# Order of the next norm in the attention steps, of one small transpose, and of four matmul groups in an attention and feed-forward layer

## The chip, the cores and the metric

One core of one Trainium2 chip runs the whole program in one launch. The metric is the time on the device in microseconds (us). Engines: PE is TensorE (matmuls and transposes), DVE is VectorE, ACT is ScalarE, POOL is GpSimd, SP is SyncE, whose queue issues most of the transfers (DMA).

## The reference

x has 2048 tokens of 1024 numbers, all float32. It is a layer with two halves:

```python
x = x + attention(layernorm(x))
x = x + ffn(layernorm(x))
# attention: q, k, v = h @ w.T + b, 32 heads of 32; per TOKEN, over the heads:
#   scores = q[h] . k[t] / sqrt(32); probs = softmax over t; context = probs @ v
# ffn: w1, w2, w3 are quantized to 16 levels (NF4) with one scale for 64 weights,
#   and dequantized; out = (silu(x @ w1.T) * (x @ w2.T)) @ w3.T, hidden size 2752
```

The attention mixes the 32 heads of one token, not the tokens. So the work of 128 tokens is independent of that of all others.

## The kernel before

**Attention.** The tokens are taken in 16 steps of 128 rows (n = 0 to 15, T = 16). In step n the projections of rows n are made, while the attention of the rows of step n-1 is finished (their second half of V's evacuation and the scores, softmax and mixing), the norm of the rows n+1 is made, and the second norm (ahead of the feed-forward part) is made of rows n-2. Each engine has its own program; they meet at semaphores only. Steps 2 to 13 are written as a loop of two steps on SP and DVE, and in full on the others.

- PE in one step (`step` in `tensor`, L1072): the first half of the scores (64 products of 32x32 for 16 of 32 tokens of a quadrant, recorded as 128), Q's first half (16 matmuls of 128x512 into one bank), the second half of the scores, Q's second half, then the wait for `normed` and the eight transposes of the next rows (`turn`, L281), K in two halves with the first mix product between them, the second mix product, and V.
- DVE in one step (`step` in `vector`, L821): V's second evacuation of the rows before, the transposition of V, one look at feed-forward weights (an absmax over blocks of 64, L813), the statistics of the next rows (`norm_stats`), the statistics of the second norm (`moments2`, whose last instruction is L263), Q's first evacuation (L799), `center(n, 0)` (row maxima and subtraction for the first half of the scores, L934 and L936), `norm_apply` (L275: (x - mean) * rstd on 128x1024 numbers in SBUF), a look, the flip of the first half of the probabilities (`flip_probs`, L951), the second norm (L942), `center(n, 1)`, and so on.
- ACT makes the exponential of each half (L1028), splits the transposed rows into a high half (L287), and makes one level of the first quantized weights after another (L1021, L1023).
- POOL in one step (`step` in `gpsimd`): the residual of rows n-2 (L766), `inv_std` (the power -0.5 of the next rows' variance, L271), `inv_std2` (the same for the second norm, L770, which waits for DVE's L263), then `add_level` three times (L760: one more level is added to 128x1024 weights). Level 0 of a unit of weights needs no addition: the first call has none in steps 1, 6 and 11.

The next rows' norm needs DVE's statistics and POOL's power. PE's transposes wait for it:

```python
def norm_apply(dve, n, slot):
    dve.wait_ge(rstd_ready, n + 1)
    nc.vector.tensor_scalar(x_nat[:, slot], x_nat[:, slot], mean_var[:, 0:1], rstd[:, 0:1],
                            ALU.subtract, ALU.mult).then_inc(normed, 1)
```

**From attention to feed-forward.** Parts of the feed-forward program run inside steps 14 and 15 and the tail. Each engine's feed-forward program is a generator; a call of `next(feed)` or `next(ahead)` runs it to its next `yield`. PE's parts are: the transposition of the four maxima of the weights (L1924, waits for `ff_max`), inside V of step 14; the spread of the four maxima to all partitions (L1927, waits for `ff_max_all`, DVE's L1754 and L1755), at the end of step 14. DVE reads the spread in step 15 (L1759); POOL's power L1553 follows.

**The opening.** Round 0 of the feed-forward part has a form of its own. Gate and up of the first tile of hidden units are made for the token blocks 0 and 1 (512 tokens each), 24 matmuls to each of the four products. The scores and mixes of the very last rows (step "T") are put between these matmuls: `gate_up` gets a slot number, counts on by one for each matmul, and `attend_last` puts the halves of the scores behind the slots 0 and 8 and the halves of the mix behind the slots 40 and 56. The first mix waits for `flip_probs(T, 0)` of DVE, the second for `flip_probs(T, 1)`. Product (m, sb_): m is 0 for gate and 1 for up, sb_ is the token block. Gate waits for the transposed weights of gate, up for those of up, and both for the tokens of the block (`x2_in`). SP's queue has, in this order, the transposition of up's weights (`turn_early(1)`), the store of x2's rows and the load of token block 1 (`load_tokens(1)`).

ACT makes silu of the two gates in the opening in a fixed order with the signs from which DVE sums up the next weights:

```python
silu(0, 0, 0, P)
silu(0, 0, 1, P)
compare(0, opening_steps[7:11], FULL)
hidden_hi(0, 0, 0, P)
```

DVE in the tail (`tail` in `vector`) has the statistics of rows 14, `center(T, 0)`, the second norm of rows 14, `flip_probs(T, 0)`, three sums, `center(T, 1)`, one sum, `flip_probs(T, 1)`, `sum_rows`, two sums, `weigh(15, 0)`, the three sums of the signs 7 to 9, `weigh(15, 1)`, the context's flip, `hidden_value` of block 0 and so on. The residual (POOL), the second norm and the turning of the last rows follow.

**Rounds.** From then on 11 rounds, each with gate and up of two tiles for four token blocks, and the down product of 16 token tiles. The weights of the next tiles are quantized meanwhile: signs on ACT (L1584), sums on DVE (L1716, L1718), scales and low halves on POOL, transposition by DMA.

Of the kernel before, what the change touches and what calls it, by code (L numbers as in the profile page):

```python
# [175 lines left out]
def attention(nc, g):  # L176
# [13 lines left out]
    with ExitStack() as mine:  # L190
# [74 lines left out]
        def norm_stats(dve, n, slot, loaded):  # L265
            dve.wait_ge(x_in[slot], 16 * loaded)
            moments(dve, x_nat[:, slot], stats, mean_var, var_eps, var_ready)
# [5 lines left out]
# [4 lines that stand above are left out]
# [513 lines left out]
        def vector(dve, feed):  # L790
            def evacuate(n, u, it, m, h):
                i = 2 * m + h
                cols = slice(h * BANK, (h + 1) * BANK)
                if m > 0 and h == 0:
                    dve.wait_ge((None, q_ready, k_ready)[m], n + 1)
                if m == 0 and h == 0 and not (it is None and n == 0):
                    dve.wait_ge(v_ready, n)
                dve.wait_ge(projected, 6 * n + i + 1)
                nc.vector.scalar_tensor_tensor(qkv[:, cols], bank[:, (6 * u + i) % PROJ_RING], un_scale[:, i:i + 1],  # L799
                                               bias[:, m, cols], ALU.mult, ALU.add).then_inc(evacuated, 1)  # L800
# [15 lines left out]
            def step(n, u, it, project=True, normalize=True, attend=True, end=True, feed=None, ahead=None):  # L816
                todo = looks(n, u, it)

                def look():
                    if todo:  # L820
                        look_at(*todo.pop(0))  # L821

                if it is not None:
                    seq.at(before_loop + it * (2 * MARKS) + u * MARKS)
                if attend:
                    evacuate(n - 1, 1 - u, it, 2, 1)
                    turn_v(n)
                    look()
                if feed:
                    next(feed)  # L830
                if normalize:
                    norm_stats(dve, n + 1, 1 - u, (n + 1) // 2 + 1 if it is None else it + 2 + u)
                if end:
                    moments2(n - 2)
                if normalize and not attend:
                    norm_apply(dve, n + 1, 1 - u)
                    look()
                if project:
                    evacuate(n, u, it, 0, 0)
                if attend:  # L840
                    center(n, 0)
                if feed:
                    next(feed)
                if normalize and attend:
                    norm_apply(dve, n + 1, 1 - u)
                look()
                if attend:
                    flip_probs(n, 0, end)
                if end:
                    norm2(n - 2)  # L850
                if attend:
                    center(n, 1)
                if project:
                    evacuate(n, u, it, 0, 1)
                if feed:
                    next(feed)
                if normalize:
                    split_lo(dve, n + 1, xT_lo[:, 1 - u], xT_hi[:, 1 - u], x_hi_done, x_lo_done)
                if attend:
                    flip_probs(n, 1, end)  # L860
                if project:
                    dve.wait_ge(evacuated, 6 * n + 2)
                    nc.vector.transpose(qT[:].rearrange("p t h u -> p h t u"),
                                        qkv[:].rearrange("p (h d) -> p h d", d=HD)).then_inc(q_ready, 1)
                if feed:
                    next(feed)
                if attend:
                    sum_rows()
                look()
                if project:  # L870
                    evacuate(n, u, it, 1, 0)
                look()
                if ahead:
                    dve.wait_ge(absmax_done, 3 * FT + 3 + 2)
                    next(ahead)
                if attend:
                    weigh(n - 1, 0)
                if project:
                    evacuate(n, u, it, 1, 1)
                    dve.wait_ge(evacuated, 6 * n + 4)  # L880
                    nc.vector.transpose(kT[:].rearrange("p t h u -> p h t u"),
                                        qkv[:].rearrange("p (h d) -> p h d", d=HD)).then_inc(k_ready, 1)
                if project:
                    evacuate(n, u, it, 2, 0)
                if feed:
                    next(feed)
                if attend:
                    weigh(n - 1, 1)
                    flip_context(n - 1)
                look()  # L890
                if it is None and n == 0:
                    invert_first()
                if ahead:
                    next(ahead)
                if it is not None:
                    assert seq.off == MARKS
                    if u == 1:
                        seq.at(before_loop + LOOP * 2 * MARKS)
# [22 lines left out]
            def turn_v(n):  # L921
                dve.wait_ge(evacuated, 6 * n)
                nc.vector.transpose(vT[:].rearrange("p t d u -> p d t u"),
                                    qkv[:].rearrange("p (d h) -> p d h", h=HEADS)).then_inc(v_ready, 1)
# [124 lines left out]
        def tensor(pe, feed_program):  # L1049
# [22 lines left out]
            def step(n, u, it, project=True, normalize=True, attend=True, end=True, feed=None, ahead=None,  # L1072
                         with_lo=False):
                def score_second():
                    score_part(n, end, HALF, QUAD)

                def mix_first():
                    mix_part(n, 0, HALF)

                def ahead_half():  # L1080
                    next(ahead)

                if project:
                    pe.wait_ge(x_lo_done, 2 * n + 2)
                    if attend:
                        score_part(n, end, 0, HALF)
                    project_one(n, u, it, 0, with_lo, score_second if attend else None)
                if normalize:
                    pe.wait_ge(normed, n + 2)
                    turn(x_nat[:, 1 - u], x_turned)  # L1090
                if project:
                    project_one(n, u, it, 1, with_lo, mix_first if attend else None)
                    if attend:
                        mix_part(n, HALF, QUAD)
                    project_one(n, u, it, 2, with_lo, ahead_half if ahead else None)
                if ahead:
                    next(ahead)

            def score_part(n, end, first, last):

                for t in range(first, last):
                    half = t // HALF
                    if t == 0:
                        pe.wait_ge(k_ready, n)
                    if t == 0:
                        pe.wait_ge(q_ready, n)
                    if t % HALF == 0 and end and scores_of(n) is scores:
                        pe.wait_ge(ctx_read, 2 * n + half - 3)
                    for rows in quadrants:
                        ins = nc.tensor.matmul(scores_of(n)[rows, t], qT[rows, t // 2, :, t % 2], kT[rows, t // 2, :, t % 2], start=True, stop=True)  # L1110
                    if t % HALF == HALF - 1:
                        ins.then_inc(scores_done, 1)
# [52 lines left out]
def feed_forward(nc, g):  # L1165
# [26 lines left out]
    with ExitStack() as mine:  # L1192
# [655 lines left out]
        def tensor(pe):  # L1848
# [62 lines left out]
            def body(r, sizes, opening=False):  # L1911
                for w in range(4):
                    if opening and w == 0:
                        for at, (m, sb_) in enumerate(((0, 0), (0, 1), (1, 0), (1, 1))):
                            gate_up(r, 0, sb_, P, (m,), True, 3 * C * at)
                        continue
                    gate_up(r, w // 2, w % 2 * 2, sizes[w // 2], opening=opening)
                    gate_up(r, w // 2, w % 2 * 2 + 1, sizes[w // 2], opening=opening)
                pe.wait_ge(w_ready, (r * 6 + 6) * 32)
                for st in range(T):  # L1920
                    down(r, st, sizes[0:GROUP])
# [34 lines left out]
```

## Time and profile before

| | us |
|---|---|
| median of 3 runs | 1895.01 (1889.67 to 1895.59) |
| the profiled execution, its own time | 1894.59 |
| its span, first to last instruction | 1892.7 |
| PE busy | 1831.2 |
| DVE busy | 1729.0 |
| ACT busy | 1378.0 |
| POOL busy | 1252.9 |
| granted TensorE clock, mean | 0.993 |

The profile is of one execution. Busy times are sums of instructions. A row of the timeline has the start in us, the duration in us, the engine, the line of the kernel, the operation with the tile written and those read, the shapes, the number of instructions that the row joins, and in square brackets how long the engine had been idle before and who released it. Starts of neighbouring instructions overlap their predecessors' ends by some 0.07 us on DVE, and matmuls overlap by design. The granted clock is given as a share of 2.4 GHz.

### The profile page before, as it was taken

The numbers are of one execution on the slowest core, as the hardware profiler recorded it, in microseconds if no ns is written. First come the engines' busy times: TensorE is split into PE (matmuls) and PEld (weight loads), VectorE is DVE, ScalarE is ACT, GpSimd is POOL, SyncE is SP. The second block draws the span as 40 slices with busy tenths as digits, with TensorE's granted clock in tenths as the row PEclk, the third lists the DMA queues.
The fourth block names the chain that finished last, engine by engine and source line by source line (L and its number), as shares of the span: only waits on it lengthen the run. The fifth ranks groups of instructions, "written<-read, shape, count | busy, mean of one in ns | idle before, by whom it ended". The sixth has DMA issues, their size and how long they took to land. (4 is left out here: it accounts for less than half of the span.)

```text
span 1892.7 us, 42748 instructions
## 1 busy us (share of the span) xinstructions
PE 1831.2 (97%) x16470; PEld 884.2 (47%) x16470; DVE 1729.0 (91%) x1848; ACT 1378.0 (73%) x1523; POOL 1252.9 (66%) x706
## 2 busy tenths in 40 slices
PE   6899999999989999999999999999999999999998
PEld 6555555555434344444444444444444444444443
DVE  6799999999888999999999999999999999999985
ACT  7233333333359898898998988989989889898881
POOL 0134534534647887977878779778787787787961
PEclk9999999999999999999999999999999999999999
DMA  9346666665587131221122212212211221131115
GB/s 322 123 128 188 169 173 198 170 174 157 133 215 239 41 66 45 45 62 49 44 52 47 56 44 50 61 44 50 61 44 44 50 61 44 44 65 42 39 29 190
DMA packets 252925, 182.76 MB, mean 97 GB/s; under 512 B 177792, under 2 KB 220800, under 8 KB 252800
## 3 DMA queue, kind: packets, MB, share of 16 engines
q1 hardware_dynamic: 221600, 167.28, 31.8%
q10 hardware_dynamic: 31200, 13.64, 3.5%
q8 instruction: 100, 1.64, 0.4%
q14 instruction: 25, 0.20, 0.0%
HBM read 114.29 MB, written 24.12 MB: 73 GB/s over the span
## 5 line engine op out<-in xcount | busy, mean ns | idle before, releaser
L1718 DVE SCALAR_TENSOR_TENSOR bank<-signs,bank 128x1024 f32<-128x1024 int8 (+2 forms) x756 | 919.9, 1217 | 53.2 <-ACT signs L1584 25.8
L1878 PE MATMUL bank<-x2T,w12T 128*128 128x512 f16 x4128 | 896.3, 380 | 8.3 <-DMA x2T<-x_lo_dram 5.9
L1878 PEld LDWEIGHTS bank<-x2T,w12T 128*128 128x128 f16 x4128 | 403.9, 98 | 497.5 <-DMA x2T<-x_lo_dram 6.4
L1584 ACT ACTIVATE signs<-w_first,compare_bias 128x1024 int8<-128x1024 f32 (+1 forms) x588 | 630.6, 1138 | 1.5 <-DVE bank L1718 1.1
L1584 ACT ACTIVATE signs<-w_last,compare_bias 128x1024 int8<-128x1024 f32 (+2 forms) x294 | 314.4, 1119 | 0.8 <-DVE w_first L1718 0.6
L1068 PE MATMUL bank<-wT,xT_hi 128*128 128x512 f16 x768 | 294.8, 384 | 2.4 <-PEq L321 2.4
L1068 PE MATMUL bank<-wT,xT_lo 128*128 128x512 f16 x768 | 294.1, 383 | 2.0 <-issue 2.0
L1906 PE MATMUL bank<-w3T_hi,hT_hi 128*128 128x512 f16 x672 | 255.3, 380 | 7.5 <-DMA w3T_lo<-half 4.7
L1907 PE MATMUL bank<-w3T_lo,hT_hi 128*128 128x512 f16 x672 | 255.4, 380 | 0.0
L1908 PE MATMUL bank<-w3T_hi,hT_lo 128*128 128x512 f16 x672 | 255.4, 380 | 0.0
L1498 POOL TENSOR_TENSOR acc<-acc,hidden 128x512 f32<-128x512 f32 x160 | 201.1, 1274 | 27.5 <-ACT hidden L1625 26.7
L1625 ACT ACTIVATE hidden<-bank,un_scale 128x512 f32<-128x512 f32 x160 | 109.3, 683 | 86.1 <-PE bank L1908 60.6
L1783 DVE SCALAR_TENSOR_TENSOR acc<-bank,un_scale,acc 128x512 f32<-128x512 f32 x192 | 143.2, 746 | 21.9 <-PE bank L1904 11.6
L1492 POOL TENSOR_TENSOR hT_lo<-hidden,hT_hi 128x512 f16<-128x512 f32 (+1 forms) x88 | 101.9, 1158 | 86.3 <-ACT hT_hi L1614 83.7
L1465 POOL TENSOR_SCALAR step_part<-w_first 128x1024 f32<-128x1024 f32 (+1 forms) x42 | 152.4, 3629 | 8.0 <-POOL w_last L1478 3.0
L1021 ACT ACTIVATE w12T<-w12T,compare_bias 128x1024 f32<-128x1024 f32 x45 | 51.7, 1149 | 141.9 <-issue 51.3
L1474 POOL TENSOR_TENSOR w_first<-w_first,step_part 128x1024 f32<-128x1024 f32 (+1 forms) x42 | 99.1, 2358 | 78.0 <-DVE w_first L1718 78.0
L1068 PEld LDWEIGHTS bank<-wT,xT_hi 128*128 128x128 f16 x768 | 75.6, 98 | 91.0 <-issue 8.7
L1068 PEld LDWEIGHTS bank<-wT,xT_lo 128*128 128x128 f16 x768 | 75.8, 99 | 83.6 <-issue 3.4
L1028 ACT ACTIVATE probs<-probs 128x512 f32<-128x512 f32 x32 | 20.1, 629 | 124.6 <-DVE probs L936 124.6
L760 POOL TENSOR_TENSOR w12T<-w12T 128x1024 f32<-128x1024 f32 x28 | 66.1, 2361 | 67.1 <-ACT w12T L1023 67.1
L1906 PEld LDWEIGHTS bank<-w3T_hi,hT_hi 128*128 128x128 f16 x672 | 65.9, 98 | 88.7 <-DMA w3T_lo<-half 5.7
(140 smaller groups left out, 2142.7 us busy)
## 6 DMA issues: line engine op xcount, KB each, us to landing
ff_raw<-in_L_ffn_w SPq DMA_DIRECT2D x63, 512.0 KB, 4.6
w_first<-in_L_ffn_w SPq DMA_DIRECT2D x41, 512.0 KB, 3.8
w_last<-in_L_ffn_w SPq DMA_DIRECT2D x19, 512.0 KB, 4.0
x_nat<-in_L_attn_hidden_states SPq DMA_DIRECT2D x16, 512.0 KB, 5.8
x_res<-in_L_attn_hidden_states SPq DMA_DIRECT2D x16, 512.0 KB, 5.3
x<-x_res SPq DMA_DIRECT2D x16, 512.0 KB, 3.6
acc<-x SPq DMA_DIRECT2D x4, 2048.0 KB, 8.2
out<-acc SPq DMA_DIRECT2D x15, 512.0 KB, 2.6
```

Source lines behind the costliest of these rows:

```text
L1068: ins = nc.tensor.matmul(to, x, w, start=j == 0, stop=j == len(passes) - 1)
L1465: nc.gpsimd.tensor_scalar(step_part[0:rows, 0:cols], w_nat(slot)[0:rows, 0:cols], float(BOUNDS[APART]), 2 * HALF_STEP[APART], ALU.is_gt, A ...
L1492: nc.gpsimd.tensor_tensor(hT_lo[0:rows, p, cols], hidden[0:rows, par], hT_hi[0:rows, p, cols], ALU.subtract).then_inc(h_lo_done[par], 1)
L1498: nc.gpsimd.tensor_tensor(acc[:, st, BANK:], acc[:, st, BANK:], hidden[:, st % 2], ALU.add).then_inc(summed, 1)
L1584: nc.scalar.activation(signs[0:rows, ring(v, k), 0:cols], w_nat(v % SLOTS)[0:rows, 0:cols], ACT.Sign, scale=COMPARE[SUMMED[k]][0], bias=co ...
L1625: nc.scalar.activation(hidden[:, st % 2], down_bank(st, 1), ACT.Copy, scale=un_scale[:, 2:3]).then_inc(down_read[1], 1)
L1718: V.scalar_tensor_tensor(to, part, HALF_STEP[SUMMED[k]], total, ALU.mult, ALU.add).then_inc(sign_used, 1)
L1783: V.scalar_tensor_tensor(acc[:, st, cols], down_bank(st, h), un_scale[:, 2:3], acc[:, st, cols], ALU.mult, ALU.add).then_inc(down_read[h], 1)
L1878: last = nc.tensor.matmul(dst, w, tokens_of(sb_, x)[:, :, c], start=c == 0 and i == 0, stop=c == C - 1 and i == 2)
L1906: nc.tensor.matmul(dst, hT_hi[k, p, toks], w3T_hi[k, p, cols], start=p == 0, stop=False)
L1907: nc.tensor.matmul(dst, hT_hi[k, p, toks], w3T_lo[k, p, cols], start=False, stop=False)
L1908: last = nc.tensor.matmul(dst, hT_lo[k, p, toks], w3T_hi[k, p, cols], start=False, stop=p == GROUP - 1)
```

## The change

Three edits, all of order; no instruction is added or taken away.

1. DVE, steps with attention and a next norm (1 to 14): `norm_apply` of the next rows stands ahead of `center(n, 0)` and not behind it.
2. PE: the spread of the maxima (L1927) was the last thing of step 14; it now stands in step 15, behind the first half of the scores.
3. PE, opening: the four products come as gate 0, up 0, gate 1, up 1 and not as gate 0, gate 1, up 0, up 1. The slots of the scores and mixes keep their numbers, so the two mixes now lie in up 0 and gate 1 and not in gate 1 and up 0.

```diff
@@ DVE, step @@
                 if project:
                     evacuate(n, u, it, 0, 0)
+                if normalize and attend:
+                    norm_apply(dve, n + 1, 1 - u)
                 if attend:
                     center(n, 0)
                 if feed:
                     next(feed)
-                if normalize and attend:
-                    norm_apply(dve, n + 1, 1 - u)
                 look()
@@ PE, step @@
                     if attend:
                         score_part(n, end, 0, HALF)
+                    if feed:
+                        next(feed)
                     project_one(n, u, it, 0, with_lo, score_second if attend else None)
...
                     project_one(n, u, it, 2, with_lo, ahead_half if ahead else None)
-                if ahead:
-                    next(ahead)
@@ PE, body of the rounds @@
                     if opening and w == 0:
-                        for at, (m, sb_) in enumerate(((0, 0), (0, 1), (1, 0), (1, 1))):
+                        for at, (m, sb_) in enumerate(((0, 0), (1, 0), (0, 1), (1, 1))):
                             gate_up(r, 0, sb_, P, (m,), True, 3 * C * at)
```

## Rows read from the trace of the kernel before

**Rows 1.** The page, busy time of each engine, share of the span, instructions.

```profile
PE 1831.2 (97%) x16470; PEld 884.2 (47%) x16470; DVE 1729.0 (91%) x1848; ACT 1378.0 (73%) x1523; POOL 1252.9 (66%) x706
```

**Rows 2.** Waits of PE, whole span: waited for, us in total, times, longest.

```profile
PE bank L1878 <- DMA x2T<-x_lo_dram: 5.9, 1, 5.9
PE bank L281 <- DVE x_nat L275: 5.4, 8, 1.0
PE bank L1906 <- DMA w3T_lo<-half: 4.7, 2, 3.1
...
PE bank L1927 <- DVE ff_raw L1755: 2.7, 1, 2.7
...
PE bank L1906 <- DVE acc L1783: 1.2, 1, 1.2
```

**Rows 3.** Waits of DVE from 120 to 466 us.

```profile
DVE qkv L799 <- PE bank L1068: 9.8, 12, 1.7
```

**Rows 4.** Timeline of DVE in step 9.

```profile
323.24 0.16 DVE L263 TENSOR_SCALAR norm_row<-norm_row 128x1 f32<-128x1 f32 x1
...
324.01 0.68 DVE L934 TENSOR_REDUCE row_max<-bank 128x16 f32<-128x512 f32 x1
324.72 0.69 DVE L936 TENSOR_TENSOR probs<-bank,row_max 128x512 f32<-128x512 f32 x1
325.33 1.57 DVE L275 TENSOR_SCALAR x_nat<-x_nat,mean_var,rstd 128x1024 f32<-128x1024 f32 x1
```

**Rows 5.** Timeline of POOL in step 9.

```profile
324.00 2.36 POOL L760 TENSOR_TENSOR w12T<-w12T 128x1024 f32<-128x1024 f32 x1
```

**Rows 6.** Timeline of step 10, the same two places.

```profile
351.76 2.35 POOL L760 TENSOR_TENSOR w12T<-w12T 128x1024 f32<-128x1024 f32 x1
351.89 0.68 DVE L934 TENSOR_REDUCE row_max<-bank 128x16 f32<-128x512 f32 x1
```

**Rows 7.** Timeline of DVE in step 6, in which POOL adds no level there.

```profile
239.49 0.80 DVE L275 TENSOR_SCALAR x_nat<-x_nat,mean_var,rstd 128x1024 f32<-128x1024 f32 x1
```

**Rows 8.** Step 15: DVE's timeline; POOL's L1540 by line (ns min/median/max, first and last start).

```profile
503.04 1.78 DVE L942 TENSOR_SCALAR x_res<-x_res,norm_row 128x1024 f32<-128x1024 f32 x1
...
L1540 POOL TENSOR_TENSOR w12T<-w12T,inv_first x2: 1901/2126/2351, 502.4 to 504.2; 128x1024 f32<-128x1024 f32 x2
```

**Rows 9.** Timeline of PE from step 14 to step 15.

```profile
491.09 0.22 PE L1927 MATMUL bank<-ident,ff_raw 4*128 4x4 f32 x1 [2.66 <-DVE ff_raw L1755]
491.30 1.87 PE L1110 MATMUL bank<-kT,qT 32*32 32x32 f32 x128
```

**Rows 10.** Timeline of all engines around the second mix of step 15.

```profile
509.94 0.65 DVE L951 STREAM_TRANSPOSE flipped<-probs 128x512 f32<-128x512 f32 x1
...
510.65 0.54 PE L1124 MATMUL bank<-vT,flipped 32*32 32x32 f32 x40
```

**Rows 11.** Timeline of PE in the opening.

```profile
525.21 3.41 PE L1878 MATMUL bank<-x2T,w12T 128*128 128x512 f16 x15
534.52 6.15 PE L1878 MATMUL bank<-x2T,w12T 128*128 128x512 f16 x17 [5.91 <-DMA x2T<-x_lo_dram]
...
548.11 0.39 PE L1124 MATMUL bank<-vT,flipped 32*32 32x32 f32 x24 [1.65 <-issue]
```

**Rows 12.** Timeline of DVE in the opening.

```profile
536.59 0.70 DVE L951 STREAM_TRANSPOSE flipped<-probs 128x512 f32<-128x512 f32 x1
...
543.45 0.70 DVE L951 STREAM_TRANSPOSE flipped<-probs 128x512 f32<-128x512 f32 x1
...
548.61 3.89 DVE L1718 SCALAR_TENSOR_TENSOR bank<-signs,bank 128x1024 f32<-128x1024 int8 x3
```

**Rows 13.** Timeline of ACT in the opening.

```profile
545.42 1.27 ACT L1607 ACTIVATE hidden<-bank,un_scale 128x512 f32<-128x512 f32 x2
```

**Rows 14.** Windows: stretch, us, busy of PE, PEld, DVE, ACT, POOL, then the granted clock.

```profile
534.00:537.00 3.00, 2.48 (x6) 0.89 (x7) 1.14 (x2) 0.35 (x2) 0.00 (x0) 0.50 1.05 402
```

**Rows 15.** Waits of DVE from 550 to 634 us.

```profile
DVE hidden L1726 <- ACT hidden L1607: 2.8, 1, 2.8
```

## The prediction

> **What bounds the kernel now.** I read the page's busy times first: PE is busy 97% of the span, DVE 91% [rows 1]. So only two things can move the time: PE's few waits, or DVE, which has little room. PE's waits come next [rows 2]. Three of them are what the three edits touch: the turn of the next rows waiting for `norm_apply` (8 times, 5.4 us in all), the spread of the maxima (2.7 us), the tokens of block 1 in the opening (5.9 us). If each vanished for good, the kernel would be 14.0 us faster. Two later ones are what such a gain has to survive: PE waits for the turned w3 weights (4.7 us, two times) and for DVE's first sum of the down product (1.2 us), both at the end of round 0 or later.
>
> Then DVE's own waits in the attention steps [rows 3]: from 120 to 466 us it waits for PE only 9.8 us in 12 waits, in some 12 steps of 28 us. The steps are a loop of two engines, each nearly full: what one loses, the other soon feels.
>
> Then one step, number 9, on DVE and on POOL, [rows 4] and [rows 5]. The move in this step is where the case is decided. `norm_apply` (L275) takes 1.57 us there, but 0.80 us in a step in which POOL adds no level [rows 7]. POOL's addition (L760) runs from 324.00 to 326.36, and `norm_apply`, recorded from 325.33, ends at 326.90, 0.54 us behind it: it has waited for POOL's instruction to end. The same is seen with L942, which began at 503.04 and took 1.78 us: it ended at 504.82, some 0.5 us behind the first of two POOL instructions (502.4, 1.90 us long), and the second of them, begun at 504.2, took 2.35 us instead of 1.90, having waited for DVE in turn [rows 8]. So these two-scalar instructions from and to SBUF and POOL's do not run together; one waits for the other.
>
> **Edit 1, the norm ahead of centring (steps 1 to 14).** Nothing is added or removed: `norm_apply` changes places with the reduce and subtract of `center(n, 0)` (0.68 and 0.69 us). If nothing stood in its way it would start 1.32 us earlier (324.01, where centring starts, instead of 325.33), which covers the longest wait of PE's turn (1.0 us).
>
> But its new start is 324.01, where centring starts now, and POOL's addition starts at 324.00; in step 10 it is 351.89 against 351.76 [rows 4 to 6]. Both hang on the same DVE instruction, the second variance at 323.24. Ten of the steps 2 to 13 have that addition (6 and 11 have none): five odd ones with a distance of 0.01 us, four even ones with 0.13, and step 2 with a larger one. If POOL is first, `norm_apply` still ends at 326.90, so PE's turn gains nothing, and DVE stands from 324.01 to 326.90: 2.89 us where it spent 1.57. That is 1.32 us more, and centring, now behind it, starts 2.8 us later than today instead of covering the wait. Ten times 1.32 is 13.2 us; in step 14 POOL's addition is over when the norm comes now, but not when it comes earlier, about 1.1 us more. Sum on DVE: 14.3 us.
>
> What of it reaches the end? At most DVE's waits for PE take it up: 14.3 less 9.8 is 4.5 us. At least nothing does: 14.3. Going through the steps one by one, with PE's waits of [rows 2] and DVE's of [rows 3] (a wait of DVE shrinks only as far as PE has not been held back itself by a later norm), I get 6.6 us taken up and 7.7 us left. I take +7.7, an estimate. Behind the norm the exponential, the flip and the mix each come later too; the first mix product on PE is 2.8 us behind its flip now, so 1.3 us more fits.
>
> The Trainium skill (SBUF — State Buffer, "Who interferes with whom") says that DVE in a two-port mode and GpSimd share one port pair, and that whoever issues first has it for the whole instruction while the other fully blocks; the two overlaps above agree with it. It says nothing of a distance of 10 ns. The Trainium skill (Perfetto Trace Analysis, "GPSIMD Engine Instruction" and "DVE / Act Engine Instruction") adds that a POOL start in the records is the first read and a DVE start comes after its prefetch has begun, which would speak for DVE in the odd steps; no row here shows it.
>
> **Edit 2, the spread behind the last first scores.** PE stands from 488.43 to 491.09 for the copy of the maxima, then does the spread and the first scores, 1.87 us [rows 9]. Put ahead, the scores (1.3 us or a little more) fill part of that wait: PE is 1.3 to 1.9 us earlier. Nobody gets it: the second flip of the last step ends at 509.94 + 0.65 = 510.59, and PE, arriving at that time, mixes from 510.65 [rows 10]; an earlier PE waits there. DVE's next reader of the spread comes no earlier either, and not later, since the spread still runs when the copy is there. I take 0 (bounds 0 and -1.9).
>
> **Edit 3, gate and up of block 0, then of block 1.** PE ends gate 0 at 534.52 - 5.91 = 528.61 and waits for block 1 [rows 11]. Now up 0 follows at once; in the code of SP's queue its weights' turn stands ahead of the load of block 1, so they are there. After 17 of its products (some 0.216 us each: 15 took 3.41), at 532.3, it comes to the first mix of the last rows, which needs the flip that ends at 536.59 + 0.70 = 537.29 [rows 12]. So PE stands 5.0 us instead of 5.9, one place later. It is through the mix (1.3 us) at 538.6; before that was 541.9. Seven products of up 0 and nine of gate 1 bring it to 542.1, where the second mix needs the flip of 543.45 + 0.70 = 544.15: mix until 545.5, and the last 15 products of gate 1 until 548.7. Then up 1 ends at 553.9 instead of some 556.9.
>
> That is PE. But ACT's two silus, at 545.42 and together 1.27 us [rows 13], are for gate 0 and gate 1, in that order and ahead of the next signs. Gate 1 is now there at 548.7, so the second silu ends at 549.4, the next sign (1.1 us) at 550.5, and DVE wants it at 548.61 [rows 12]: 1.9 us lost. If TensorE's clock falls in the pause (the granted clock was 0.50, the lower level of 1.2 GHz, after the pause of 5.9 us [rows 14]) and the pause of 1.65 us that PE had inside the second mix [rows 11] stays, it is 3.9. I take +2.5. DVE is full from there on, and its next long wait, 2.8 us for a silu [rows 15], is at the end of a chain that runs from DVE over POOL and ACT and so moves along. PE's 3 us gained end in the waits for w3 and for DVE's sum [rows 2]. Bounds: +3.9, and -3.3 if PE and not DVE sets that place.
>
> **Sum.** 1894.6 (the profiled execution; its span is 1892.7) + 7.7 + 0 + 2.5 = 1904.8. The median of the runs is 0.4 above the profiled one: 1905.
>
> **Rivals.** About 0.3% (5.7 us) is what a measurement of this kernel can tell from no change.
> (a) Chance 0.45: POOL first in all ten steps, as summed: 1905, from 1901 (4.5 + 1.9) to 1911.
> (b) Chance 0.30: in the five odd steps DVE gets in first. There the norm takes 0.80 instead of 1.57 us and ends 2.1 us earlier, the turn never waits; the even steps lose 1.32 each. Through the steps that leaves PE and DVE 1.6 to 2.5 us earlier, less the opening: +0.9 to 0, 1896, from 1892 to 1899. For it: 0.01 us is nothing. Against: where evacuation waits for PE, DVE comes later still.
> (c) Chance 0.17, the other side: DVE is first nearly everywhere. The turn's 5.4 us go and DVE saves up to 7.7 (ten times 0.77), enough to follow. With +2.5 of the opening that is 1892; with the opening and the spread paying too (3.3 and 1.3), 1885. It decides from the point at which `norm_apply` is let in before a POOL instruction started 0.13 us earlier.
> (d) Chance 0.08: the norm waits as in (a), but the DVE and PE waits take up nearly all, and silu is not in the way: 1895, give or take 4.
>
> Slower by over 0.3%: (a) and a little of (b), 0.47. Faster: most of (c), 0.16. Within: 0.37. The range, 1889 to 1909, leaves out the best of (c) and the top of (a). The likeliest case alone is 1901 to 1911.
>
> **What would show it.** Right: L275 of 2.7 to 2.9 us in ten steps, each ending 0.54 behind L760; PE's turn still waits for it, in more steps; DVE's waits for PE in the steps nearly gone; silu of gate 1 waits for PE and DVE's sums wait for signs near 549. The spread's wait is near 1.3, with a new wait at the mix. Wrong: L275 of 0.80 in steps with an addition, with L760 longer instead; then (b) or (c). If L275 is 2.9 and the time is the same, the step that fails is what the waits take up.

## The result and the profile after

| | before | after |
|---|---|---|
| median, us | 1893.61 (4 runs, 1889.67 to 1895.59) | 1917.49 (4 runs, 1916.44 to 1921.58) |
| span of the profiled execution | 1892.7 | 1919.8 |
| start of the spread (L1927) | 491.1 | 506.4 |
| from there to the end | 1401.6 | 1413.4 |

The changed kernel takes 1.0133 times as long as before (95% interval 1.0109 to 1.0156): 24 us slower, where 10 were forecast and the range ended at 15 above the time before. The spread of the maxima is a good place to cut the time in two: in the traces, up to it 15.3 us are lost, behind it 11.8. That makes 27 us and not 24: the profiled execution (1921.58) was the longest of the four.

DVE in step 9, the stretch of [rows 4]; columns as in every timeline row:

```profile
332.13 0.15 DVE L263 TENSOR_SCALAR norm_row<-norm_row 128x1 f32<-128x1 f32 x1
332.23 0.75 DVE L799 SCALAR_TENSOR_TENSOR qkv<-bank,scales,bias 128x512 f32<-128x512 f32 x1
332.90 2.88 DVE L275 TENSOR_SCALAR x_nat<-x_nat,mean_var,rstd 128x1024 f32<-128x1024 f32 x1
335.70 0.68 DVE L934 TENSOR_REDUCE row_max<-bank 128x16 f32<-128x512 f32 x1
```

And POOL in the same step, which answers to [rows 5]:

```profile
332.37 0.55 POOL L770 TENSOR_TENSOR norm_row<-norm_row,power 128x1 f32<-128x1 f32 x1 [1.20 <-DVE norm_row L263]
332.89 2.34 POOL L760 TENSOR_TENSOR w12T<-w12T 128x1024 f32<-128x1024 f32 x1
```

The norm starts 0.01 us behind POOL's addition and ends at 335.78, 0.55 us after the addition's end (335.23). It has waited for all of it, and centring stands behind it. In all 17 traces, wherever a norm starts with 0.3 us or more of an addition left, it ends 0.55 us behind the addition's end.

Nine of the ten steps look like this: L275 takes 2.88 us in the steps 3, 5, 7, 9 and 13, 2.75 to 2.77 in 4, 10 and 12, and 2.52 in 2. The tenth, step 8, is the odd one on DVE:

```profile
299.28 0.15 DVE L263 TENSOR_SCALAR norm_row<-norm_row 128x1 f32<-128x1 f32 x1
303.25 0.75 DVE L799 SCALAR_TENSOR_TENSOR qkv<-bank,scales,bias 128x512 f32<-128x512 f32 x1 [3.82 <-PE bank L1068]
303.92 0.80 DVE L275 TENSOR_SCALAR x_nat<-x_nat,mean_var,rstd 128x1024 f32<-128x1024 f32 x1
```

DVE stood 3.82 us for PE, POOL's addition was over, and the norm took 0.80.

PE's waits from 100 to 500 us, first before, then after (waited for, us in total, times, longest). "issue" is a pause in which PE waited for nothing that the profile shows:

```profile
PE bank L1110 <- issue: 3.7, 3, 1.8
PE bank L1124 <- issue: 2.9, 3, 1.3
...
PE bank L1068 <- issue: 2.0, 2, 1.2
```

```profile
PE bank L1110 <- issue: 7.0, 4, 3.0
PE bank L281 <- DVE x_nat L275: 5.6, 7, 2.0
PE bank L1124 <- issue: 5.4, 4, 2.0
PE bank L1068 <- issue: 4.7, 2, 2.7
```

The turn still waits for the norm, 5.6 us (5.4 in [rows 2]). The pauses without a releaser have doubled, from 8.6 to 17.1 us. How much of that is scatter, the traces with the same attention code tell: they have 8.6, 9.1 (the kernel before), 7.8, 9.7 (edit 3 without edit 1) and 12.8 us (edit 2 alone); the five with edit 1, no wait on POOL and full loads have 16.3 to 17.7.

Where the pauses stand, the order of PE's records shows (matmuls, weight loads and its sequencer's, numbered from the start). The first of them in all four of before, edit 1 alone, the longer DVE below and the changed kernel stands before record 3777, at 147 to 149 us. All 151 pauses without a releaser from 100 to 500 us in the 17 traces stand a multiple of 256 records from it, give or take one or two. So they are not unnamed waits for a result of DVE, ACT or POOL, which could end before any record: they belong to places in PE's program.

DVE's waits for PE, which were to take up part of the loss, have grown too, from 9.8 us [rows 3] to 15.2 (from 120 to 482 us, the same steps):

```profile
DVE qkv L799 <- PE bank L1068: 15.2, 10, 3.9
```

The opening on PE, which answers to [rows 11]:

```profile
541.85 7.08 PE L1878 MATMUL bank<-x2T,w12T 128*128 128x512 f16 x32
553.68 1.83 PE L1124 MATMUL bank<-vT,flipped 32*32 32x32 f32 x121 [4.75 <-issue]
559.88 0.33 PE L1124 MATMUL bank<-vT,flipped 32*32 32x32 f32 x7 [4.36 <-issue]
560.14 6.18 PE L1878 MATMUL bank<-x2T,w12T 128*128 128x512 f16 x16
566.24 1.44 PE L1124 MATMUL bank<-vT,flipped 32*32 32x32 f32 x128
```

Up 0 now follows gate 0 at once (32 matmuls in a row). The first mix starts when its flip is done (552.88 + 0.70 = 553.58): the 4.75 us are that wait, whatever the bracket says (and it is at no multiple of 256 records). Seven products before the mix's end comes a pause of 4.36 us, which is at one. The granted clock was at its lower level all that time (window, us, busy of PE, PEld, DVE, ACT, POOL, clock):

```profile
552.00:565.00 13.00, 6.95 (x140) 3.76 (x141) 12.45 (x14) 6.77 (x7) 6.07 (x3) 0.50 0.96 246
```

And this is what it does to ACT and to DVE, one row of each, against [rows 13] and [rows 12]:

```profile
571.06 0.69 ACT L1607 ACTIVATE hidden<-bank,un_scale 128x512 f32<-128x512 f32 x1 [8.66 <-PE bank L1878]
```

```profile
572.82 1.23 DVE L1718 SCALAR_TENSOR_TENSOR bank<-signs,bank 128x1024 f32<-128x1024 int8 x1 [7.83 <-ACT signs L1584]
```

The second silu stands 8.66 us for gate 1, and DVE 7.83 us for the sign behind it.

### The profile page after: what moved, and what is told of

The parts are those of the page before. It is cut to its first block and busy times, and to the rows that moved or that the text cites. A ratio compares the mean times of both kernels' runs of the same rounds, so it can differ in the third digit from the quotient of the medians.

```text
span 1919.8 us, 42748 instructions
## 1 busy us (share of the span) xinstructions
PE 1841.3 (96%) x16470; PEld 887.5 (46%) x16470; DVE 1740.8 (91%) x1848; ACT 1377.3 (72%) x1523; POOL 1252.9 (65%) x706
## 5 line engine op out<-in xcount | busy, mean ns | idle before, releaser
L1878 PEld LDWEIGHTS bank<-x2T,w12T 128*128 128x128 f16 x4128 | 404.7, 98 | 497.4 <-issue 11.8
L1068 PE MATMUL bank<-wT,xT_lo 128*128 128x512 f16 x768 | 298.4, 389 | 4.8 <-issue 4.7
L1068 PE MATMUL bank<-wT,xT_hi 128*128 128x512 f16 x768 | 299.3, 390 | 2.4 <-PEq L321 2.4
```

The costliest lines, as they stand in the source:

```text
L1068: ins = nc.tensor.matmul(to, x, w, start=j == 0, stop=j == len(passes) - 1)
L1878: last = nc.tensor.matmul(dst, w, tokens_of(sb_, x)[:, :, c], start=c == 0 and i == 0, stop=c == C - 1 and i == 2)
```

## The experiments

The table cuts each traced execution at the spread. The ratio is to the kernel before on the same chip. Differences in us in the text are of medians where nothing else is said; the interval belongs to the ratio, and the two can differ by up to 2 us.

| kernel | spread at | from there to the end | ratio, 95% interval |
|---|---|---|---|
| before, second trace | 490.4 | 1402.0 | |
| edit 2 | 495.4 | 1403.5 | 0.9996 (0.9984 to 1.0008) |
| edit 3 | 488.9 | 1409.9 | 1.0037 (1.0024 to 1.0049) |
| edit 3, silu later | 488.9 | 1403.3 | 1.0009 (0.9995 to 1.0024) |
| edit 1 | 504.4 | 1402.7 | 1.0071 (1.0053 to 1.0090) |
| edit 1, POOL waits | 486.7 | 1402.5 | 0.9981 (0.9971 to 0.9991) |
| before, POOL waits | 489.3 | 1402.3 | 1.0007 (0.9993 to 1.0022) |
| before, small loads | 482.7 | 1404.0 | 0.9980 (0.9966 to 0.9994) |
| edit 1, small loads | 495.7 | 1402.9 | 1.0034 (1.0021 to 1.0047) |
| before, DVE longer | 508.2 | 1404.3 | 1.0090 (1.0067 to 1.0113) |
| edits 1 and 3 | 507.0 | 1412.5 | 1.0121 (1.0098 to 1.0144) |
| all three, again | 505.1 | 1410.4 | 1.0133 (1.0115 to 1.0152) |
| all, silu later | 507.6 | 1404.2 | 1.0093 (1.0066 to 1.0121) |
| all, POOL waits | 486.4 | 1411.8 | 1.0004 (0.9992 to 1.0017) |
| all, POOL waits, silu later | 483.9 | 1404.6 | 0.9989 (0.9978 to 1.0000) |

**Edit 1 alone (norm_only).** The first hunk of the diff.

> Edit 1 alone. Theory P (the norm stands behind POOL's addition, and the lost time is multiplied by PE's longer pauses and the clock that falls in them): L275 takes 2.75 to 2.9 us in nine or ten steps, the attention steps end 12 to 15 us later, and the kernel is 12 to 18 us slower than before. Rival O (the opening loses it all): within 5 us of before.

1.0071, 12.6 us by the medians. The attention part is 13.3 us later, the rest within 1.1 us of before. The pauses of PE are 16.3 us. L275 takes 2.75 to 2.9 us in eight steps, 2.52 in step 2 and 1.74 in step 3, and here step 14 is among the eight (2.89 us, POOL's addition 1 ns ahead). P holds, O falls.

**Edit 2 alone (spread_only).** The second hunk.

> Edit 2 alone. Both theories: PE's wait for the copied maxima falls from 2.7 to some 1.3 us, a new wait of the same size stands before the second mix of step 15, and the time is that of before within 2 us.

The time is as expected. PE's waits from 488 to 540 us:

```profile
PE bank L1124 <- DVE flipped L951: 2.4, 1, 2.4
...
PE bank L1927 <- DVE ff_raw L1755: 1.4, 1, 1.4
```

The wait for the copy has halved, and a new one stands before the mix, 2.4 us and not the 1.3 expected.

**Edit 3 alone (gates_only).** The third hunk.

> Edit 3 alone. Theory S (the second silu waits for gate 1 and holds up the signs): DVE waits 2 to 8 us for signs after weigh(15, 0), the kernel is 3 to 10 us slower. Rival N (edit 3 loses only because edit 1 has moved the transfers under it): DVE's wait is under 2 us and the time within 3 us of before.

Slower by 6.1 us in the medians. The part behind the spread is 8.3 us longer, and DVE waits 7.4 us for signs: S, at the upper end.

**The port taken out of edit 1 (norm_pool_waits).** Edit 1 and, on POOL:

```diff
+                if normalize and attend:
+                    pool.wait_ge(normed, n + 2)
                 if attend:
                     add_level(n, 0)
```

> Edit 1, and POOL's first addition of a step waits until the norm is done, so that the two never overlap. Theory P: L275 takes 0.80 us in every step, PE's turn no longer waits for it (5.4 us before), and the kernel is 2 to 8 us faster than before. Rival C (it is the later centring, not the port, that costs): as slow as edit 1 alone within 3 us.

Step 9 in its trace, DVE and POOL (line numbers two higher from here on in that kernel):

```profile
320.02 0.81 DVE L275 TENSOR_SCALAR x_nat<-x_nat,mean_var,rstd 128x1024 f32<-128x1024 f32 x1
320.74 0.68 DVE L936 TENSOR_REDUCE row_max<-bank 128x16 f32<-128x512 f32 x1
```

```profile
320.91 2.36 POOL L762 TENSOR_TENSOR w12T<-w12T 128x1024 f32<-128x1024 f32 x1 [0.86 <-DVE x_nat L275]
```

L275 takes 0.79 to 0.81 us in all 16 steps, PE's turn waits no more, and the kernel is faster than before by 0.19%, clear of its interval: the only one here that does the whole work and is. With the same order on DVE, one wait on POOL turns 12.6 us lost into 4.5 gained. P holds, C falls.

**The same wait in the kernel before (before_pool_waits).** Norm behind centring, POOL waits for it.

> The kernel before, with POOL's first addition of a step waiting for the norm, which stands behind centring as before. L275 takes 0.80 us everywhere, which saves DVE ten times 0.7. Theory P (the port): PE's turn waits less than 5.4 us since the norm ends 0.7 us earlier; the kernel is 1 to 4 us faster, less than with the norm ahead of centring (4.5). Rival C: within 1 us of before.

1.0007 (0.9993 to 1.0022), a miss: the norm takes 0.80 us everywhere and the turn waits 1.2 us instead of 5.4, yet nothing is gained. DVE's norms take 6.8 us less in steps 2 to 13, and none of it arrives. PE's pauses without a releaser are 12.7 us there, 8.6 before; but 12.8 were also seen with unchanged attention code, so that the pauses ate the gain is possible and not shown. The time is within the 1 us that rival C gave here; it is the run before, where C fell by over 10 us, that decides against it. Of the two, only both together, the POOL wait and the earlier norm, pay.

**Are the pauses tied to the loads? (before_small_loads, norm_small_loads).** In the load of the looks, inside the loop only (both kernels leave out part of the scales by it):

```diff
+                if rows == P and not isinstance(j, int):
+                    sp.dma_start(ff_raw[0:rows, slot, 0:E // 8], (w1, w2, w1)[m][bass.ds(first, rows), 0:E // 8]).then_inc(ff_in[slot], 16)
```

> The kernel before, with the looks' loads of feed-forward weights in steps 2 to 13 cut to an eighth (512 to 64 KB each; the absmax is then of old data, so the scales are left out in part). Theory F (PE's pauses without a releaser are instruction fetches that stand behind these loads): the pauses from 100 to 480 us fall from 8.6 to under 4 us and the kernel is 1 to 4 us faster. Rival G (they do not hang on the loads): the pauses stay at 7 to 10 us, the time within 2 us.

> The same cut in the kernel with edit 1 alone. Theory F: against the kernel before with the cut it is 6 to 10 us slower, which is the port alone (the 7.7 of the prediction), since the pauses and the falls of the clock are gone; L275 still takes 2.75 to 2.9 us in ten steps. Rival G: 12 us slower or more, as without the cut (12.6).

In the kernel before, the pauses from 100 to 480 us fall from 8.6 to

```profile
PE bank L1112 <- issue: 2.8, 2, 2.1
```

and the kernel is faster (0.9980, 0.9966 to 0.9994). F's first expectation holds: the pauses hang on the loads. The busy share of the DMA engines falls with them, from 0.61 (126 to 466 us) to 0.42 (124 to 458); which of the other transfers that relieves, this does not tell. With edit 1 the pauses are 5.8 us and the ratio is 1.0034 (1.0021 to 1.0047). Between the two lie 10.1 us, at the edge of what F expected, and in the traces the spread is 13.0 us later (482.7 and 495.7). The norms of edit 1 cost DVE 12.5 us more in these traces, and PE's turn feels it directly:

```profile
PE bank L281 <- DVE x_nat L275: 8.3, 11, 1.1
```

```profile
PE bank L281 <- DVE x_nat L275: 12.4, 10, 2.1
```

DVE's waits for PE were 3.7 us without edit 1 and 4.5 with it. So with the pauses mostly gone, what the port costs on DVE arrives nearly in full, and DVE's waits do not shrink. The first of these numbers says one thing more: of the 9.8 us that DVE waits for PE in the kernel before, 6 went with the pauses. So most of that reserve seems to have been an echo of PE's pauses; what the smaller loads change besides them, this pair can't separate.

**DVE's time alone (dve_longer).** The kernel before with a reduce behind the norm in steps 2 to 13:

```diff
+                if it is not None:
+                    nc.vector.tensor_reduce(g["top_all"][:, 0:1], bias[:, 0], AX.X, ALU.max)
                 look()
```

> The kernel before, with one more reduce of 1.2 us on DVE behind the norm in each of steps 2 to 13 (its result is not used): DVE's time alone, 14 us in all, without the port and without a later norm in the step itself. Theory D (DVE's lost time comes through in full, since PE's pauses grow by what DVE's waits would take up): 11 to 15 us slower. Rival A (the absorption of the prediction, 6.6 of 14.3): 5 to 9 us slower.

1.0090 (1.0067 to 1.0113), which is 17.0 us (12.7 to 21.4), 18.7 by the medians; the spread is at 508.2. Twelve reduces of 1.21 us are 14.5 us. All of it arrives; whether more does, the interval leaves open. The time lies above D's range, so its size is a miss. PE's pauses are 18.6 us, DVE's waits for PE 12.7: they did not shrink here either. That nothing is taken up holds; A falls. The other direction is different: the 6.8 us taken from DVE with the POOL wait alone (above) brought nothing.

**Silu later (gates_silu_later).** Edit 3 alone, and on ACT:

```diff
             silu(0, 0, 0, P)
+            compare(0, opening_steps[7:10], FULL)
             silu(0, 0, 1, P)
-            compare(0, opening_steps[7:11], FULL)
+            compare(0, opening_steps[10:11], FULL)
```

> Edit 3 alone, and ACT makes the signs 7 to 9 ahead of the silu of gate 1 and not behind it. Theory S: DVE's wait of 7.4 us for signs falls under 2 us, and of the 6.1 us by which edit 3 is slower 4 or more go (within 2 us of before, or faster). Rival M (PE's longer pauses in the two mixes set the end themselves): still 4 us slower or more.

ACT in its trace:

```profile
544.17 0.69 ACT L1607 ACTIVATE hidden<-bank,un_scale 128x512 f32<-128x512 f32 x1
544.76 3.21 ACT L1584 ACTIVATE signs<-w_first,compare_bias 128x1024 int8<-128x1024 f32 x3
552.68 0.69 ACT L1607 ACTIVATE hidden<-bank,un_scale 128x512 f32<-128x512 f32 x1 [4.71 <-PE bank L1879]
```

PE's wait for the flip and its pause in the first mix are as long as with edit 3 alone (4.9 and 4.4 us, 5.1 and 4.4 there), the silu of gate 1 still waits, but the three signs no longer do. DVE's wait for signs is 1.2 us in all, and the part behind the spread is 1403.3 us. S holds, M falls.

**All three once more, and without edit 2 (after_again, norm_gates).**

> The changed kernel itself, beside its parts on one chip. If the parts add up (12.6 for edit 1, 6.1 for edit 3, about 0 for edit 2) it is 18 to 19 us slower than before; the first measurement gave 24, so by a rival they strengthen each other and it is 22 or more.

> Edits 1 and 3 without edit 2. If edit 2 is nothing here as it is alone: within 2 us of the changed kernel. Rival: edit 2 does harm beside the others (the waits it moves meet the fetches): 3 us or more faster than the changed kernel.

25 and 24 us slower. Edit 2 does nothing here either. The medians of the parts (12.6, 6.1, -1.1) add up to 17.6 only, so by the medians the rival (22 or more) holds. By the ratios the parts add up to 19.7 us, with some 5 us either way, and the whole is 25.2 (21.8 to 28.8): that they strengthen each other is likely and not shown.

**Each cause taken out of the whole (after_silu_later, after_pool_waits, norm_waits_all), and before once more.**

> The changed kernel with the signs 7 to 9 ahead of gate 1's silu. Theory S (what edit 3 costs beside edit 1 is the same wait for signs): DVE's wait of 7.8 us goes and the kernel is 12 to 16 us slower than before, near edit 1 alone (12.6). Rival J (the two edits join in another place): 18 us slower or more.

> The changed kernel with POOL's first addition behind the norm. Edit 3 then costs what it costs with an early attention: 6 to 8 us from the 4.5 gained, so 1 to 4 us slower than before. Rival J (edit 3 costs 11 us whenever edit 1 is there): 6 us slower or more.

> All three edits, with POOL's first addition behind the norm and the signs 7 to 9 ahead of gate 1's silu. Both causes taken away: 2 to 7 us faster than before (4.5 from the norm, minus the 2 that edit 3 costs even so, and 0 to 3 that the earlier spread may give). If there is a third cause of the slowdown, it is slower than before.

> The kernel before once more, for its trace: how far the place of the spread (491.1 us in the first trace, 488.9 in two kernels with the same attention code) differs between executions. Expected within 488 and 492 us, so that differences of 2 us between single traces say nothing.

With silu later, 18.5 us remain of 25 (17.6 by the ratio, 12.5 to 22.9): more than the 16 of the expectation, and at the border of rival J, which the interval neither confirms nor rules out; DVE's wait for signs fell from 8.6 to 1.9 us. With POOL waiting, 0.8 us remain: less than expected, and here rival J (6 us or more) falls. With both, it is 1.8 us faster than before, less than expected, with an interval that touches 1; there is no sign of a third cause. In the traces the parts look like this: behind the spread edit 3 adds 8 to 12 us whenever the silu stands where it stood, and 1 to 3 if not. The attention part is at 504.4 to 507.6 with edit 1, and at 488.9 to 491.1 without it in four traces, but at 495.4 in that of edit 2 alone, whose code is the same up to there. The repeated trace of the kernel before (490.4) was within the 488 to 492 expected of it. So single traces scatter by some us, and that of edit 3 alone reached the spread 2.2 us early. The late one, edit 2's, is of an execution that took 6 us more than its median, and has 12.8 us of pauses.

## Why the prediction was wrong

- **POOL first in all ten steps, case (a): right**, in nine of ten, the odd steps at a distance of some 10 ns too. L275's 2.75 to 2.9 us, its end 0.54 us behind the addition, and the turn that still waits, are as stated. Step 8 escaped, and the 1.1 us of step 14 did not come (0.81 us); in edit 1 alone they did. On DVE this is 11.2 us and not 14.3.
- **What of it reaches the end: the step that failed.** "I get 6.6 us taken up and 7.7 us left." Of DVE's loss nothing was taken up: the spread is 13.3 us later in edit 1 alone and 15.3 in the changed kernel, for 12.1 and 11.2 us more on DVE. The step took PE's program as fixed, so that DVE's waits for PE were a reserve. They did not shrink: 9.8 us became 15.2, 12.7 with the longer DVE. Most of them seem to be an echo of PE's pauses (3.7 us are left with the small loads), and the pauses doubled. TensorE's clock was at its lower level for 20.5 us between 100 us and the spread, where it was 3.4 before. That DVE's time alone arrives in full is shown by dve_longer; that it does nearly so even without most pauses, by the small loads. Growing waits and pauses are no sign of a slower kernel by themselves: edit 1 with POOL's wait has 14.2 and 13.8 us of them and is 4.5 us faster.
- **Edit 2: right**, 0, with the new wait before the mix.
- **Edit 3: the mechanism right, the size wrong.** The first mix's wait (5.0 forecast, 4.75 measured), the silu in the way and the chain from DVE on are as stated. The term was +2.5, at most 3.9; it was 8 to 12. The second silu was forecast at 549.4, which is 565.7 on the changed kernel's clock (16.3 us later at the flip); it ended at 571.75, 6 us behind. The mis-sized parts are two. The pause inside the mix, taken over as 1.65 us from another place, was 4.36, in a stretch in which the DMA engines were 0.96 busy. And the clock stayed at 0.50 for 13.7 us and not for 6.8, which can cost PE up to 3.4 us more (an estimate, half of the difference).
- **PE's 3 us of gain in the opening: wrong.** They never came. The last of the 96 products ends at 576.2 in the changed kernel, 15.8 us behind the second flip (560.45); before, it ended at 557.0, 12.9 us behind that flip (544.15). The wait for block 1 is gone, but the pause and the clock took more. So the claim that DVE and not PE sets the opening was not tested by a faster PE. What the silu experiment shows is that DVE's wait for signs is what edit 3 cost: with the signs free it costs nothing that can be measured (0.9995 to 1.0024).
- Direction and case were right, the time was not: the bounds of the terms came from rows of a kernel with fewer pauses, and even the largest of them (14.3 and 3.9) add up to 18 us, where 24 were measured.

Open: why PE's pauses grow when DVE is late, and when PE is earlier as well. That they stand at multiples of 256 records and shrink with the loads speaks for the instruction fetches of theory F; the trace does not show a fetch, so this is an inference.

## What to carry to other kernels

Before an instruction of DVE that works from SBUF to SBUF is moved, look at what POOL starts at its new place: in this kernel one semaphore wait on POOL decided between 12.6 us lost and 4.5 gained. Where two engines are both nearly full, do not count the waits of one for the other as a reserve: here 6 of 9.8 us went away with the other engine's pauses, and none took up a loss. A test with one added instruction prices a microsecond more on an engine better than a sum of waits, but not a microsecond less: 14.5 us added cost 17, 6.8 us removed gained nothing. When matmul groups change places, follow every consumer that takes their results in a fixed order, and ask what is queued behind the one that is now late.

## What the runs showed of the hardware

- A start of POOL some 10 ns ahead of DVE's in the records (332.89 and 332.90) was enough for POOL in every such step of the six traces with edit 1 and no wait on POOL (the recorded distances are 9 to 16 ns); once 1 ns was (477.95 us in edit 1 alone). The prediction's thought that DVE could win these ties is not borne out. No trace has DVE ahead by so little, so what such a lead would do is not shown.
- Pauses of PE without a releaser went from 8.6 to 2.8 us when loads of 512 KB were cut to 64 KB, and were 16 to 19 us when DVE was made later. All from 100 to 500 us, in every trace, stand at multiples of 256 PE records (give or take one or two) from each other.
- The clock fell to its lower level during or shortly behind pauses of PE of 1.8 to 5 us (in the changed kernel at 148.9 us, behind one of 2.70; at 224.0, behind one of 1.98; at 295.7, within one of 3.02; in the kernel before at 460.7, behind one of 1.81), 3.4 to 13.7 us each time, but not at every one: the changed kernel has another of 1.98 at 364.9 us without a fall. Up to 700 us the changed kernel spent 58 us there in 11 stretches, the kernel before 24 in 5.
